# First FFN of a macaron layer: eleven token tiles scattered before the others, four full blocks first in the table, the folding of the attention's weights moved behind the positions, and the attention's weights sent during the blocks

## What is computed

```python
x = x + 0.5 * ffn(_layernorm(x))          # FFN 0
x = x + attn(_layernorm(x))
x = x + 0.5 * ffn(_layernorm(x))          # FFN 1

def ffn(x):                                # 8 experts, one chosen for each token
    probs = softmax(x @ w_router); sel = argmax(probs); wgt = probs[sel]
    for e in range(8):
        y = relu(x @ w1[e] + b1[e]) @ w2[e] + b2[e]      # 128 -> 512 -> 128
        out += where(sel == e, wgt, 0)[:, None] * y
def attn(x):
    xn = layernorm(x) * ln_g + ln_b
    x_t = xn @ W_up_l.T + b; r_t = xn @ W_up_r.T + b; x_c = silu(conv4(x_t))
    skip, q, k, i, f from x_c;  v, o from x_t             # projections with W_skip, W_q, W_k, W_i, W_f, W_v, W_o
    ...                                                    # gated linear recurrence over 512 tokens, head norm
    return ((hn + skip) * silu(r_t)) @ W_down.T + b + x
```

## Time and profile before

| | |
|---|---|
| runs | 484.71, 485.36, 488.89 us; median 485.36 |
| the profiled execution | 484.73 us, of which the traced span is 482.9 us |
| busy | PE 80%, weight loads 67%, DVE 71%, ACT 45%, POOL 36% of the span |
| the chain that ended last | PE 45%, DVE 27%, issue 10%, ACT 9%, DMA 4% |
| granted TensorE clock, mean | 0.92 of 2.4 GHz |

### The profile page before, as it was taken

How to read it: one execution, slowest core, us unless ns; L and a number is a source line. 1 busy time by engine, 2 the same in 40 slices (tenths; PEclk the granted TensorE clock), 3 DMA queues, 4 the chain that set the end, 5 groups by cost and what they waited for, 6 DMA issues and landing times.

```text
span 482.9 us, 10042 instructions
## 1 busy us (share of the span) xinstructions
PE 386.2 (80%) x2986; PEld 323.4 (67%) x3003; DVE 342.8 (71%) x1015; ACT 216.5 (45%) x557; POOL 172.9 (36%) x158
## 2 busy tenths in 40 slices
PE   5447999906999897999898998898999983199980
PEld 5322999904777676877676777676777873199970
DVE  3692677667449979659789579789498688567763
ACT  2641344424454563545573455474555640144430
POOL 4374244521004435105433114542024317735450
PEclk9999799957999998999999999999999955589995
DMA  9992122169900000000000000000000400222216
GB/s 293 374 361 60 35 67 65 54 202 359 335 16 1 1 1 1 1 1 0 0 0 0 0 0 0 0 0 0 0 1 2 174 2 33 60 57 70 68 49 180
DMA packets 25660, 35.32 MB, mean 73 GB/s; under 512 B 3521, under 2 KB 17729, under 8 KB 25121
## 3 DMA queue, kind: packets, MB, share of 16 engines
q1 hardware_dynamic: 21554, 26.24, 16.9%
q0 software_dynamic: 2496, 5.13, 3.1%
q10 hardware_dynamic: 1584, 3.63, 2.2%
HBM read 17.52 MB, written 17.47 MB: 72 GB/s over the span
## 4 chain that ended last, share of the span: by engine, by line
PE 45%; DVE 27%; issue 10%; ACT 9%; DMA 4%; POOL 2%; SPq 1%; DVEq 1%; ACTq 0%; POOLq 0%
PE bank L856 41%; ACT WVT L749 2%; ACT E L758 2%; DVE CS L1810 2%; DMA QKT<-by_token 2%; DVE W1R L1832 1%; DVE HS L1834 1%; PE bank L973 1%; PE bank L1084 1%; DVE X L1301 1%; DVE FL L1741 1%; PE bank L877 1%; DMA by_token<-YB,IDX 1%; DVE CS L1811 1%; DVE AG L1742 1%
## 5 line engine op out<-in xcount | busy, mean ns | idle before, releaser
L519 POOL DMA_INDIRECT by_token<-YB,IDX x46 | 44.0, 957 | 58.3 <-DVE YB L1542 57.7
L856 PE MATMUL bank<-XBT,W1R 128*128 128x128 f32 x368 | 52.5, 289 | 1.1 <-DVE W1R L1530 1.0
L749 ACT ACTIVATE WVT<-bank,AC 128x128 f32<-128x128 f32 x128 | 36.6, 375 | 30.6 <-PE bank L856 30.2
L856 PEld LDWEIGHTS bank<-XBT,W1R 128*128 128x128 f32 x368 | 47.8, 203 | 2.3 <-ACT XBT L655 1.4
L856 PE MATMUL bank<-W,HT 128*128 x368 | 49.2, 277 | 0.0
L856 PEld LDWEIGHTS bank<-W,HT 128*128 128x128 f32 x368 | 45.3, 194 | 0.3
L545 POOL TENSOR_TENSOR HS<-HS,MHALF 128x8 f32<-128x8 f32 x11 | 18.1, 1643 | 70.8 <-DVE HS L1842 70.8
L713 ACT ACTIVATE QKT<-bank,COLS 128x512 f32<-128x512 f32 x32 | 22.0, 687 | 41.5 <-PE bank L856 41.5
L495 POOL DMA_INDIRECT slots<-XN,POS x32 | 31.5, 985 | 16.6 <-issue 16.6
L1796 DVE TENSOR_TENSOR WOT<-bank,WVT 128x512 f32<-128x512 f32 x32 | 21.9, 685 | 20.4 <-ACT WVT L749 20.3
L526 POOL TENSOR_TENSOR LA<-LA,MHALF 128x8 f32<-128x8 f32 x4 | 8.0, 2002 | 77.1 <-DVE LA L1688 77.1
(11 more groups left out here) (342 smaller groups left out, 1027.5 us busy)
## 6 DMA issues: line engine op xcount, KB each, us to landing
slots<-FILL SPq DMA_DIRECT2D x37, 258.0 KB, 6.2
W<-w SPq DMA_DIRECT2D x2, 2048.0 KB, 8.0
XB<-slots SPq DMA_DIRECT2D x46, 64.5 KB
W<-w SPq DMA_DIRECT2D x1, 2064.0 KB
QKT<-by_token SPq DMA_DIRECT2D x8, 256.0 KB, 4.1
slots<-QKT SPq DMA_DIRECT2D x1, 1483.5 KB, 11.2
X<-x SPq DMA_DIRECT2D x4, 256.0 KB, 5.2
out<-X SPq DMA_DIRECT2D x4, 256.0 KB, 2.5
```

The source lines that it names most:

```text
L519: g.indirect_dma_start(out=by_token[f], out_offset=bass.IndirectOffsetOnAxis(ap=IDX[:, j:j + 1], axis=0), in_=YB[:, j, :], in_offset=None) ...
L749: ins = a.activation(DT[:, hf, m, :], DM[:, m * P:(m + 1) * P], ACT.Exp, bias=AC[:, c, h:h + 1])
L856: return t_.matmul(o, l, r, start=start, stop=stop, skip_group_check=True)
```

## The change

In words:

1. POOL's 16 scatters stay as they are, but the first eleven count a semaphore of their own (`scattered_soon`). SP's first four loads wait for these eleven alone, block 4 for the other five.
2. A new function `first_blocks` on DVE makes the table of FFN 0 as FFN 1 does: the first four blocks are full ones made of the first eleven tiles (eleven tiles always have four), the others follow. SP reads each block's row from SBUF.
3. DVE's order: `fold_weights` (TZ, WCT, FOLD: the start of the old `attn_setup`) comes right behind the positions, then `first_blocks`, `skip_bias`, `gate_masks`, the rest of `attn_setup`. `small_weights` goes behind the first block's index, `shares` behind the blocks.
4. ACT copies the first two experts' weights (`W1R`, `B2R`) in DVE's place, before it rounds folded weights. It sends the attention's weights one by one in the first four turns of the blocks. `SELQ` is made after the blocks in `split_weights`, and PE waits for it before the first q projection.

```diff
+SOON, FEW = 11, 4
@@ over_blocks
             for j in range(RING):
                 turn(j, j, 0)
+                if after:
+                    after(j)
@@ SP
                 def row_of(k):
-                    if f == 1:
-                        return sp.value_load(ROWNO[0:1, bass.ds(k, 1)], min_val=0, max_val=(NSLOT - 1) * P)
-                    return k * P
+                    return sp.value_load(ROWNO[0:1, bass.ds(k, 1)], min_val=0,
+                                         max_val=((NSLOT if f else NBLK) - 1) * P)
...
+                    if f == 0 and j == FEW - RING:
+                        sp.wait_ge(scattered[f], 16 * (NT - SOON))
...
+                sp.wait_ge(eid_ready[f], 1)
+                first = [row_of(j) for j in range(RING)]
                 if f == 0:
-                    sp.wait_ge(scattered[f], 16 * NT)
+                    sp.wait_ge(scattered_soon, 16 * SOON)
@@ POOL
-                    scatter(0, 0, NT, scattered[0])
+                    scatter(0, 0, SOON, scattered_soon)
+                    scatter(0, SOON, NT, scattered[0])
@@ ACT
                     exponentials(0)
-                    for dst, src in ((WQT[:, :, :], wqt), (WKT[:, :, :], wkt), (WSKT[:, :, :], wskt),
-                                     (WDT[:, :, :], wdt)):
-                        act.dma_start(dst, src).then_inc(attn_loaded, 16)
...
-                    act.wait_ge(picks_ready, 1)
-                    a.activation(SELQ[:, :, :].rearrange("p c (h s) -> p (c h) s", h=H),
-                                 PICK[:, :, :].rearrange("p c h -> p (c h)").unsqueeze(2).to_broadcast([P, NC * H, P]),
-                                 ACT.Copy).then_inc(constants_cast, 1)
-
+                    act.wait_ge(ffn_loaded, 48)
+                    act.wait_ge(eid_ready[0], 1)
+                    for k in range(2):
+                        e = act.value_load(EID[0:1, k:k + 1], min_val=0, max_val=NE - 1)
+                        a.activation(B2R[:, k, :], B2[:, e, :], ACT.Copy)
+                        a.activation(W1R[:, k, :], W1[:, e, :], ACT.Copy).then_inc(w1_copied[0], 1)
                     act.wait_ge(fold_full, 2)
...
-                over_blocks(act, turn)
+                def load_attention(j):
+                    dst, src = ((WQT[:, :, :], wqt), (WKT[:, :, :], wkt), (WSKT[:, :, :], wskt), (WDT[:, :, :], wdt))[j]
+                    act.dma_start(dst, src).then_inc(attn_loaded, 16)
+
+                over_blocks(act, turn, after=None if f else load_attention)
@@ PE
             pe.wait_ge(w_low, 1)
+            pe.wait_ge(constants_cast, 1)
             head_qk(0, WQH, WQL, "q", lambda: head_carry(0), 3)
@@ DVE
                     first_route()
-                    shares(0)
+                    fold_weights()
+                    first_blocks()
+                    skip_bias()
+                    gate_masks()
                     attn_setup()
-                    dve.wait_ge(ffn_loaded, 48)
...
+            def first_blocks():
+
+
+                full_blocks(FEW)
+                did(v.tensor_tensor(CT[:, 9, :], EB[:, 0, :], CT[:, 2, :], ALU.subtract))
+                did(v.tensor_tensor(CT[:, 7, :], EB[:, 0, :], CT[:, 4, :], ALU.subtract))
+                step.settle()
+                table(0, FEW, CT[:, 3, :])
+                do(v.tensor_tensor_scan(CT[:, 8, :], const("ones")[:, 0:NE], CT[:, 7, :], 0.0, ALU.mult, ALU.add))
+                did(v.memset(CT[:, 9, NE - 1:NE], 0.0))
+                did(v.tensor_copy(CT[:, 9, 0:NE - 1], CT[:, 4, 1:NE]))
+                step.settle()
+                table(FEW, NBLK - FEW, CT[:, 8, :])
+                do(v.tensor_scalar(ROWF[:, FEW:NBLK], ROWF[:, FEW:NBLK], CT[:, 4, 0:1], None, ALU.add))
+                numbers(0, 0, NBLK)
...
-                copy_w1(0, 0)
-                copy_w1(1, 1)
                 if f == 1:
+                    copy_w1(1, 0, 0)
+                    copy_w1(1, 1, 1)
                     late_blocks()
                 copy_idx(0, 0)
+                if f == 0:
+                    small_weights()
                 relu(0, 0)
```

## The result

| | before | after |
|---|---|---|
| median of 20 runs each | 485.98 us | 488.23 us |
| ratio after/before, 95% interval | | 1.0054, 1.0036 to 1.0072 |
| profiled execution: time, span | 484.73, 482.9 us | 487.93, 486.1 us |
| positions ready (start of POS) | 22.26 | 23.71 |
| first up, behind the positions | 27.1 | 28.3 |

The change was forecast at 480.2 us, in a range of 478.3 to 483.3; it came out 0.54% slower than before. The span grew by 3.2 us: 1.45 before the positions, 1.15 from there to the first up, where 5.2 were to be gained, 2.4 in the ring of blocks, less 1.8 behind it (1.6 of that in the attention, where profiles of one kernel differ by as much).

What follows compares the result with a forecast made beforehand. A serial DVE and PE chain, with POOL's scatters almost as long, set the blocks' start; DVE becomes the bound. First up moves from 49.39 to 44.2, nothing given back: 485.36 - 5.2 = 480.2 us, range 478.3 to 483.3.

Steps and rivals of the forecast that it cites:

- BIF at 40.5: Before FFN 0's first block: DVE, running without its 8 us pause, reaches BIF at 40.5 us.
- the start moves by 5.2 us: FFN 0's first up comes at 44.2 us instead of 49.39, a gain of 5.2 us.
- Stall: 0, at worst 0.2: In FFN 0's ring, PE's wait at block 4 for its tokens was put at 0, at worst 0.2 us.
- DVE's new chain: From the positions to the first transpose, DVE's reordered work was priced to reach BIF at 40.55 and the transpose at 43.4.
- PE's fold: Before the first block, PE's weight folding runs from 25.94 to 38.6 us, 1.2 ahead of bif, no longer setting the start.
- start later: Rival, chance 0.13: low clock in the fold or late weight copies delay the start; gain 4.4 or 3.5, time 481.0 to 481.9.
- 12.64 at most: Length of PE's weight folding before the first block, taken as at most 12.64 us.
- Scatters, W1R, SELQ, shares: Scatters allow a transpose at 41.9; W1R adds no wait; SELQ's 3.62 and shares' 0.9 us fit in idle time.
- the distance from the first up to XTH: Sign over FFN 0's blocks: 60.8 us before; the prediction is wrong if it grows.
- same start, given back in the ring: Rival, chance 0.10: block 4 comes 2 us late, PE's clock falls, 3 to 4 us go; 483 to 484.5.
- slower: Rival, chance 0.05: XB loads queue behind all weights, block 4 is 10 us late; time 490.7.
- A new median should lie as the old one: For the whole kernel: the median stands 0.63 above the profiled execution, so 485.36 less 5.2 gives 480.2 us.

Runs made afterwards that it cites:

- e5: The kernel after, unchanged, measured a second time; ratio to before 0.9963 (0.9931 to 0.9994).
- e7: The kernel after with the four sends of the attention's weights put back behind the softmax's exponentials; ratio to before 0.9857 (0.9801 to 0.9913).
- e13: The kernel after, unchanged, timed again on one more chip; ratio to before 0.9970 (0.9933 to 1.0006).
- e15: The kernel after with the four sends of the attention's weights at the old place, once more; 476.86 us, one run.
- e6: The kernel before, unchanged, profiled again; 482.57 us, one run.
- e16: The kernel after, unchanged, one more look; 490.19 us, one run.
- e17: The kernel after with the four sends of the attention's weights at the old place and a second time in the blocks; 489.30 us, one run.
- e8: e7 with the scaling of bif moved forward, right behind HEADS in gate_masks, after a wait for DVE's own operations; ratio to before 0.9855 (0.9801 to 0.9909).
- e9: The kernel after, unchanged, once more; 484.41 us, one run.
- e10: The kernel after with only the first send (WQT, 0.5 MB) in the blocks, the other three at the old place; ratio to before 0.9919 (0.9878 to 0.9961).
- e2: The kernel before with only the sends of the attention's weights moved into the first four turns of the blocks; ratio to before 1.0080 (1.0052 to 1.0107).
- e4: The kernel after with SP's four reads of row numbers behind the wait for eleven tiles; ratio to before 0.9949 (0.9915 to 0.9983).
- e14: The kernel of e4, unchanged, once more; 482.38 us, one run.
- e11: The kernel after, unchanged, one more look; 480.11 us, one run.

## Why the prediction was wrong

Two steps failed, and one term was missing. In the recorded pair most of the miss is the start: "BIF at 40.5" and with it "the start moves by 5.2 us". BIF came 24.6 us behind the positions instead of 18.3, and the first up 1.15 us later than before's instead of 5.2 earlier, because of the slow stretch. The other step is "Stall: 0, at worst 0.2": the ring takes 2.4 us longer than before's, and this one failed in every profile of after, with the stretch or without. The missing term is the moment of the positions, 1.45 us.

**DVE's new chain: right without the slow stretch, 6.35 us too early with it.** In the prediction's numbers less the positions' 22.26: BIF at 18.3, the first transpose at 21.1, the first up at 21.9. Measured without the slow stretch 17.7, 20.5 and 21.3 (e5, e7, e13, e15), so the gain was 6.2 against e6 and not 5.2; most of the difference is the bias matmuls, 0.38 us instead of 0.7, and e6's own start at 27.5. The durations taken from FFN 1 held for all 26 operations of the table: 27.50 to 33.66 in after is 6.16 against 6.06. In after, e16 and e17 the stretch lies behind these operations, on the masks.

**PE's fold: right in most, not in all.** Forecast end 16.3 behind the positions; in most profiles the last matmuls begin at 15.1 to 15.8 and take 0.6. In after, e8, e9 and e10 it was the rival "start later", by the low level; priced there at a first up 22.7 behind the positions, it came to 22.7 (e9) and 23.7 (e8, e10). "12.64 at most" was no bound: in after these matmuls took 16.35 us (27.09 to 43.44).

**Scatters, W1R, SELQ, shares: right.** XB could be used from 18.9 to 19.4 (forecast 19.6), the first up came 0.82 behind the transpose (0.81), and the join shows none of SELQ's 3.60. The last five scatters follow each other at 1.27 us in after as in before, so the slip of 0.04 us each is not seen.

**"Stall: 0, at worst 0.2": the step that failed in the ring.** I costed the sends by what they take from ACT, four issues, and compared bytes with a mean DMA share of 0.22. The term should have been how long a load of XB takes beside them, 5.5 us, against the 3.0 between its send and its use. Its price is 1.5 to 4.4 us in the ring (after's six profiles, 47.9 to 50.8, against e7's 46.4), the upper end where PE's pause also cost the clock. What PE's rows show as waits for XB is 0.7 (e13) to 2.4 us (e5) of it. The prediction's own sign, the distance from the first up to XTH, grew from 60.8 to 63.1 us (51.99 to 115.07). This is the rival "same start, given back in the ring", which had exactly this mechanism at 3 to 4 us and a chance of 0.10; where no slow stretch came, it was what happened, and 483 us the time (e5, e13). The rival "slower" did not happen: no load of XB was held for 10 us. (Its sum adds 10.5 where its own working has 10; nothing hangs on it.)

**"A new median should lie as the old one": 1.0 us off.** In all twelve profiles of kernels with a send in the blocks the positions come at 23.2 to 24.2, in all eight of the others at 22.3 to 22.9. It isn't the sends' traffic, since they are issued later than that, nor their absence from the old place, since e17 has them there too. In after w_router landed later (PE's first matmul at 6.55 instead of 5.19), in e2, e4 and e14 x did. What in the program does it is open.

**The slow stretch: in no term, and the largest part of the recorded miss.** It puts 6.4 us on DVE. Without it the fold at the low level would have held after's start at 23.7, as in e8, so it cost 4.6 there. The recorded difference of +2.25 us and e5's -1.9 lie 4.1 apart, about that. Its sign was in the trace of before, in FFN 1, on which the forecast's prices rested; five sends there, with before's second profile under it:

```profile
419.45 6.58 SPq L422 DMA_DIRECT2D XB<-slots  x5
```

```profile
417.98 4.71 SPq L422 DMA_DIRECT2D XB<-slots  x5
```

The prediction took durations from the rows of FFN 1 and asked nothing of SP's steps and DVE's longer waits between them, since nothing waited for them there.

The sum of the first pair, in us of the span: -5.2 forecast, 6.35 for the start, 2.4 for the ring, 1.45 for the positions, less 1.8 behind it: 3.2, the growth of the span. The kernel of e1 and e7, after with its sends left where they were, keeps the start, has neither the ring's loss nor the late positions, and beats both: 4.1 and 6.35 us under before, against 5.2 forecast.

## What to carry to other kernels

Price a transfer moved beside a ring by the latency it gives the ring's own loads against the time between their send and their use, not by mean DMA share; and add the clock if the engine that waits is PE. When one edit of several moves bulk traffic from a place where it was hidden, leave that edit out unless a wait there names it. When a short profile disagrees with its working by microseconds on operations that wait for nothing, profile the kernel before again on the same chip before looking for the cause in the edit.

## What the runs showed of the hardware

- A state in which SP's register operations take 0.70 us each in straight code behind a read from SBUF (four sends 5.05 us instead of 1.90), and DVE's waits for its own operations take 1.1 to 2.5 us on the same grid, while POOL's scatters keep their pace of 1.27 us. It shows in FFN 1 of all five, and in FFN 0 only of the kernels that read rows there. Five profiles, of two occasions, had it; the other fifteen had not.
- The moment at which the granted clock rises in one and the same stretch of matmuls differs by profile, so that the fold's last matmuls begin 12.8 to 18.7 us behind the positions. A row of the table of stretches that lies ahead of the trace's first record of the clock reads 1.00 for want of a record: in after, whose record begins at 57.13 us, the row of 52 to 54 us reads 1.00 with 9 matmul records, as few as at 0.50 in e7 (9 in 44 to 46). There the count decides. The 1.00 of 36 to 38 us in the earlier trace rows is such a row too, since before's record begins at 40.40.
- A pause of PE of 2.40 us was followed by a fall of the granted clock to 0.50 (e5); pauses of 2.0 and 2.1 us by none (e9, e11).
